# q of two attention tiles in single passes from the split tiles, the projection in q's bank

## The chip, the core and the metric

The kernel runs on one core of a Trainium2 chip, in one launch. The metric is the device time in microseconds from launch to end. The median of three runs of the kernel before is 2429.7 us (2426.54 to 2429.95).

## The reference

x has the shape 8 x 256 x 56 x 56 in float32. Two layers are applied, each with a residual around it and a group normalisation of 32 groups in front:

```
x = x + conv3x3(gn(x))          # 256 -> 256 channels
x = x + attention(gn(x))
```

The attention works in windows of 4 x 4 tokens. For each window:

```
qkv = qkv_w @ x                              # 768 channels, 16 tokens
msq = concat(qkv, avg_pool5(qkv))            # 64 heads of 3*8
q, k = relu(...), relu(...); v = pad(v, 1.0)
kv  = k^T v ; out = q kv ; out = out[:-1] / (out[-1] + 1e-15)
y   = batch_norm(proj_w @ out)
```

avg_pool5 is a 5 x 5 sum around each token inside its window of 4 x 4, over 25.

## The kernel before

All five engines run a program of their own, written out by hand; they meet only at semaphores. Each engine takes its instructions strictly in the order written, and a wait holds up all that stands behind it.

**Convolution.** Each image is done in 4 chunks of 14 rows, each chunk in 4 products (`product`, L332). A product is, for each half of the output channels, 18 matmuls of 392 columns: every operand is split into a high and a low part that TensorE takes in one pass (type float32r), and high x high, high x low and low x high are added. The first chunk of the next image, and a few products after it, are laid between the attention's setup and its last turns.

**Attention.** The 196 windows of an image are cut into 25 tiles of 8 windows, 128 tokens (the last tile has 4 windows). TensorE goes through them in turns s = 0 to 24 (`tile`, L429). Turns 1 to 20 are a hardware loop of ten rounds with two turns each. A turn s does, in this order:

- `attend` for tile s (L405), q times the masked kv, into BANK_O;
- `keys_times_values` for tile s+1 (L391);
- `q_of_tile` for tile s+2 (L371): plain float32 from xh, the normalised tile, into BANK_Q. A float32 matmul is two instruction pairs, so a tile has 8 matmul instructions of 128 columns;
- `turn`, the transposes of tile s (L425), from ao into BANK_O;
- `pooled` for tile s+2 (L380), the 5 x 5 sums of keys and values as a matmul over tokens, into BANK_KV;
- `project` for tile s-1 (L416), 16 matmul instructions of 128 columns, into columns from Y0 on of BANK_A and BANK_A+1;
- `keys_values` for tile s+3 (L364): 6 single passes of 512 columns from xt (the split tile) and wkv, into BANK_KV. It waits for xh_low (the tile's low part) and for vp_raw, ScalarE's last copy of the pooled product out of that bank.

ScalarE goes through `attention` (L703) in turns of the same number: pooled_q for tile s+1 (L678, waits for GpSimd's qsum), turned for tile s (L698, the transposes out of BANK_O), pooled_keys_values for tile s+2 (L652, L655; L655 signals vp_raw), q_of_tile for tile s+2 (L662 copies q to qraw, L666 writes relu(q) to qs straight from the bank), batch_norm for tile s-1 (L690), split_tile for tile s+4 (L632, the high part of xt), keys_values for tile s+3 (L639, L642, L644).

VectorE per turn: the reciprocals and outputs of tile s (L989, L991, L999), the low part of keys and values (L981), two masks of kv (L1008), normalising tile s+4 into xh (L968) and its low part (L976).

GpSimd per turn: spread_pooled for tile s+2 (L1171, waits for vp_raw), pool_q for tile s+2 (L1142 to L1161, eight additions that sum q over 5 x 5 neighbours, waits for qraw; the last one signals qsum_ready), add_tile for tile s-1 (L1182, the residual).

`at_slot` puts nops in front of a stage so that it begins at a given place of TensorE's instruction fetch block.

## Time and profile before

| | before |
|---|---|
| median of the runs | 2429.7 us |
| profiled execution | 2429.06 us |
| its span, first to last instruction | 2427.2 us |
| TensorE busy | 2367.6 us, 98% |
| VectorE busy | 1730.9 us, 71% |
| ScalarE busy | 1453.5 us, 60% |
| GpSimd busy | 1180.7 us, 49% |
| mean granted TensorE clock | 0.998 |

PE is TensorE's matmuls, PEld its weight loads, DVE is VectorE, ACT is ScalarE, POOL is GpSimd. A matmul's end is modelled, so a block's length is best taken from its start to the next block's start. Busy shares are means over stages with different limits. A small wait that ends last in a repeated turn counts more than a large one beside it.

### The profile page before, as it was taken

The page shows a single profiled execution, that of the slowest core. Times are in us where ns is not written, and L with a number is a line of the kernel's source. Part 1 is how long each engine was busy: PE and PEld are TensorE (multiplying, and loading weights), DVE is VectorE, ACT ScalarE, POOL GpSimd, SP SyncE. Part 2 cuts the span into 40 slices and gives each one's busy share as a digit, 9 for nine tenths or more (in the row PEclk, how much of TensorE's full clock was granted, in tenths as well). Part 3 has the DMA queues.
Part 4 walks back from the last instruction along what each step waited for, and adds up shares of the span by engine and source line. Part 5 has one row for each costly group of instructions (what it writes and reads, how often), then busy time and mean ns, then how long its engine had stood idle before and what let it go on. Part 6 is the DMA issues. An engine that isn't in the chain of part 4 may idle for free.

```text
span 2427.2 us, 112385 instructions
## 1 busy us (share of the span) xinstructions
PE 2367.6 (98%) x49576; PEld 2152.7 (89%) x49576; DVE 1730.9 (71%) x3202; ACT 1453.5 (60%) x3756; POOL 1180.7 (49%) x2371
## 2 busy tenths in 40 slices
PE   6999999999999999999999999999999999998998
PEld 6998889888898889988899888998889988897887
DVE  8887658776587675877658766687766876664764
ACT  2148861588615885168841788327882288813886
POOL 2027760377504774047730577206771167712776
PEclk9999999999999999999999999999999999999999
DMA  4000010000100002000010000100001000000000
GB/s 170 1 2 16 16 67 12 2 16 19 65 10 2 19 16 74 1 6 16 19 70 1 6 19 16 71 1 10 16 20 66 1 9 19 21 9 1 16 16 25
DMA packets 38826, 58.37 MB, mean 24 GB/s; under 512 B 4672, under 2 KB 36032, under 8 KB 36288
## 3 DMA queue, kind: packets, MB, share of 16 engines
q1 hardware_dynamic: 38592, 55.27, 6.4%
q8 instruction: 144, 2.36, 0.4%
q14 instruction: 90, 0.74, 0.1%
HBM read 29.57 MB, written 25.69 MB: 23 GB/s over the span
## 4 chain that ended last, share of the span: by engine, by line
PE 96%; DVE 2%; issue 1%; DMA 0%; ACT 0%; POOL 0%; SPq 0%; POOLq 0%; DVEq 0%
PE ps L345 34%; PE ps L416 15%; PE ps L364 11%; PE ps L405 10%; PE ps L391 9%; PE ps L371 9%; PE ps L380 4%; PE ps L425 3%; PE ps L327 0%; DVE dp L875 0%; DVE st L1073 0%; DMA xs<-x 0%; PE ps L356 0%; DVE kv_part L981 0%; DVE rcp L991 0%
## 5 line engine op out<-in xcount | busy, mean ns | idle before, releaser
L345 PE MATMUL ps<-dp,wc 128*128 128x392 f32 x4608 | 842.4, 342 | 4.0 <-issue 4.0
L345 PEld LDWEIGHTS ps<-dp,wc 128*128 128x128 f32 x4608 | 816.9, 188 | 9.2 <-issue 7.6
L1171 POOL TENSOR_TENSOR ve<-vpraw,vmask 128x1024 f32<-128x1024 f32 x200 | 381.0, 1905 | 352.8 <-ACT vpraw L655 352.8
L416 PEld LDWEIGHTS ps<-at,wp 128*128 128x128 f32 x3200 | 373.2, 192 | 48.3 <-DVE kvm L1008 46.4
L416 PE MATMUL ps<-at,wp 128*128 128x128 f32 (+1 forms) x3200 | 404.6, 280 | 1.7 <-ACT yb L690 1.0
L626 ACT CAST dp<-dt 128x896 fp32r<-128x896 f32 x128 | 121.1, 946 | 463.2 <-PE ps L345 374.5
L1142 POOL TENSOR_TENSOR qm<-qraw 128x64 f32<-128x64 f32 x200 | 59.6, 298 | 687.3 <-ACT qraw L662 686.8
L364 PE MATMUL ps<-wkv,xt 128*128 128x512 f32 x1200 | 324.6, 406 | 1.6 <-issue 1.6
L644 ACT ACTIVATE ve<-ps,vmask 128x256 f32<-128x256 f32 x800 | 315.0, 492 | 0.0
L405 PEld LDWEIGHTS ps<-kvm,qs 64*32 64x32 f32 x25088 | 233.6, 105 | 91.4 <-issue 89.6
L1008 DVE TENSOR_TENSOR kvm<-ps,hm 128x576 f32<-128x576 f32 (+1 forms) x400 | 277.5, 735 | 2.9 <-PE ps L391 2.9
L968 DVE TENSOR_SCALAR xh<-xs,gn 128x128 f32<-128x128 f32 (+3 forms) x560 | 278.3, 551 | 1.6 <-PE ps L371 1.3
L405 PE MATMUL ps<-kvm,qs 64*32 64x36 f32 x25088 | 260.7, 204 | 18.3 <-issue 17.7
L976 DVE TENSOR_TENSOR xt<-xh,xt 128x256 fp32r<-128x256 f32 x200 | 108.2, 541 | 236.4 <-ACT xt L632 236.3
L888 DVE TENSOR_TENSOR xs<-xs,ps 128x392 f32<-128x392 f32 x384 | 200.3, 557 | 99.1 <-PE ps L345 98.4
L1182 POOL TENSOR_TENSOR xs<-yb,xs 128x128 f32<-128x128 f32 (+3 forms) x560 | 201.8, 387 | 114.6 <-ACT yb L690 114.6
L391 PE MATMUL ps<-ve,kr 64*32 64x144 f32 x12544 | 246.3, 285 | 1.0 <-issue 1.0
L364 PEld LDWEIGHTS ps<-wkv,xt 128*128 128x128 f32 x1200 | 211.8, 189 | 37.5 <-issue 2.6
L678 ACT ACTIVATE qs<-qsum,qmaskp 128x256 f32<-128x256 f32 x400 | 182.2, 504 | 88.1 <-POOL qsum L1161 88.1
L371 PEld LDWEIGHTS ps<-xh,wq 128*128 128x128 f32 x1600 | 194.4, 191 | 43.3 <-issue 41.3
L989 DVE TENSOR_SCALAR den<-ps 128x64 f32<-128x64 f32 (+1 forms) x200 | 44.5, 223 | 261.5 <-PE ps L405 261.5
L371 PE MATMUL ps<-xh,wq 128*128 128x128 f32 x1600 | 230.2, 287 | 0.0
(86 smaller groups left out, 3121.1 us busy)
## 6 DMA issues: line engine op xcount, KB each, us to landing
out<-xs SPq DMA_DIRECT2D x224, 112.0 KB, 1.8
xs<-x SPq DMA_DIRECT2D x14, 1344.0 KB, 7.5
xs<-x SPq DMA_DIRECT2D x2, 1568.0 KB, 8.4
xs<-x SPq DMA_DIRECT2D x14, 224.0 KB, 2.7
xs<-w_conv SPq DMA_DIRECT2D x2, 1152.0 KB, 13.3
kvm<-w_kv SPq DMA_DIRECT2D x1, 512.0 KB, 14.9
wp<-w_proj SPq DMA_DIRECT2D x4, 128.0 KB, 9.5
wq<-w_q SPq DMA_DIRECT2D x1, 256.0 KB, 14.3
```

What stands on the lines that cost most here:

```text
L345: last = nc.tensor.matmul(ps[:, conv_bank(v, mt), 0:CONV_N], wc[:, part_w, k, kt * TAPS + dy, mt * P:(mt + 1) * P], dp[:, kk % 2, part_d, ...
L364: last = nc.tensor.matmul(ps[0:TT, BANK_KV, :], xt[:, part_x, e, kt, :], wkv[:, part_w, kt, :], start=(i == 0 and kt == 0), stop=(i == len ...
L371: last = nc.tensor.matmul(ps[:, BANK_Q, mt * TT:(mt + 1) * TT], wq[:, kt, mt * P:(mt + 1) * P], xh[:, e, kt, :], start=(kt == 0), stop=(kt ...
L391: last = nc.tensor.matmul(ps[32 * q:32 * q + 32, BANK_A + 2 * h + r, gg * PLACES * QW:(gg + 1) * PLACES * QW], kr[64 * r:64 * r + 64, e, k ...
L405: last = nc.tensor.matmul(ps[32 * c:32 * c + 32, BANK_O + r, (u * G + g) * QW:(u * G + g + 1) * QW], qs[64 * r:64 * r + 64, g, e, w * 32:w ...
L416: last = nc.tensor.matmul(ps[:, BANK_A + mt, Y0:Y0 + n], wp[:, q, mt * P:(mt + 1) * P], at[:, q, e, 0:n], start=(q == 0), stop=(q == QUADS ...
L644: last = nc.scalar.activation(ve[:, t % 2, e, 0].rearrange("p (n m) -> p n m", m=DIM + 1)[:, :, 0:DIM], ps[0:TT, BANK_KV, C:2 * C].rearran ...
L888: last = nc.vector.tensor_tensor(pair[:, :, e], pair[:, :, e], ps[:, conv_bank(v, mt), 0:CONV_N], op)
L968: last = nc.vector.tensor_scalar(xh[:, t % 2, kt, first * TOK:(first + n) * TOK].rearrange("p (w r c) -> p w r c", r=WS, c=WS), xs_row(b, ...
L1008: nc.vector.tensor_tensor(kvm[:, h, 0:n].rearrange("p r (g c) -> p r g c", g=2), ps[:, BANK_A + 2 * h:BANK_A + 2 * h + n, 0:2 * PLACES * Q ...
L1171: nc.gpsimd.tensor_tensor(ve[:, t % 2, :, 1].rearrange("p e (n m) -> p e n m", m=DIM + 1)[:, :, :, 0:DIM], vpraw[:].rearrange("p (n m) -> ...
L1182: last = nc.gpsimd.tensor_tensor(xrow, yb[:, t % 2, mt, first * TOK:(first + n) * TOK].rearrange("p (w r c) -> p w r c", r=WS, c=WS), xrow ...
```

## The change

- q is computed for a pair of tiles at a time, in single passes like keys and values: 3 part combinations x 2 input halves x 2 output halves, 12 matmuls of 256 columns a pair. Its inputs are the split tiles xt, which are laid out so that the two tiles of a pair stand side by side, and wq, which is split into a high and a low part at the start. An image has 13 pairs; in the last only 64 tokens are computed.
- TensorE computes q in even turns, at the place where it was; in odd turns the projection stands at that place, ahead of the transposes. In even turns the projection stays behind pooled. In turn 24 the convolution's product moves behind the transposes.
- The projection writes into BANK_Q. It waits until ScalarE has copied q out of that bank, and q_of_pair waits for batch_norm's y_ready.
- ScalarE copies a pair's q to qraw (128x512) in q_of_pair, and writes relu(q) to qs for each tile from qraw. In even turns its order is pooled_q, q_of_pair, turned, pooled_keys_values, q_of_tile, batch_norm; in odd turns it is pooled_q, q_of_tile, batch_norm, turned, pooled_keys_values.
- GpSimd's pool_q runs once a pair, over buffers of twice the width; spread_pooled stays once a tile, and in even turns pool_q still stands behind it.
- The convolution's products use other banks in two places, and three of the fetch offsets are other numbers.

```diff
@@ conv_bank
     if (c, kk) == (1, 0):
-        return (BANK_KV, BANK_Q)[mt]
-    if (c, kk) == (1, 2):
-        return BANK_O + mt
+        return (BANK_KV, BANK_C[0][1])[mt]
...
-SLOT_LEAD, SLOT_FIRST, SLOT_LOOP, SLOT_OUT = 152, 80, 92, (80, 56)
+SLOT_LEAD, SLOT_FIRST, SLOT_LOOP, SLOT_OUT = 160, 80, 92, (88, 40)
...
-        wq = sb("wq", [P, KT, C])
+        wq = sb("wq", [P, 2, KT, C], F32R)
...
-        xt = sb("xt", [P, 2, 2, KT, TT], F32R)
-        qraw = sb("qraw", [P, MT * TT])
+        xt = sb("xt", [P, 2, KT, 2, TT], F32R)
+        qraw = sb("qraw", [P, MT * 2 * TT])
...
-            def q_of_tile(e):
+            def q_of_pair(tokens=2 * TT):
                 for mt in range(MT):
-                    for kt in range(KT):
-                        last = nc.tensor.matmul(ps[:, BANK_Q, mt * TT:(mt + 1) * TT],
-                                                wq[:, kt, mt * P:(mt + 1) * P], xh[:, e, kt, :],
-                                                start=(kt == 0), stop=(kt == KT - 1))
+                    for i, (part_w, part_x) in enumerate(PARTS):
+                        for kt in range(KT):
+                            last = nc.tensor.matmul(
+                                ps[:, BANK_Q, mt * 2 * TT:mt * 2 * TT + tokens],
+                                wq[:, part_w, kt, mt * P:(mt + 1) * P],
+                                xt[:, part_x, kt, :, :].rearrange("p e t -> p (e t)")[:, 0:tokens],
+                                start=(i == 0 and kt == 0), stop=(i == len(PARTS) - 1 and kt == KT - 1))
                 last.then_inc(q_done, 1)
...
@@ project
-                        last = nc.tensor.matmul(ps[:, BANK_A + mt, Y0:Y0 + n],
+                        last = nc.tensor.matmul(ps[:, BANK_Q, mt * TT:mt * TT + n],
...
@@ tile
-                elif is_tile(2):
-                    pe.wait_ge(q_ready, n2)
-                    q_of_tile(e)
...
+                if e == 0:
+                    if is_tile(2) and s != 0:
+                        if is_tile(3):
+                            pe.wait_ge(xh_low, n4)
+                        pe.wait_ge(y_ready, n0)
+                        q_of_pair(2 * TT if is_tile(3) else TT // 2)
+                elif is_tile(-1):
+                    pe.wait_ge(qraw_ready, pairs)
+                    if is_tile(-2):
+                        pe.wait_ge(y_ready, n0)
+                    project(1 - e, 2)
+                if half and s == TILES - 2:
+                    pe.wait_ge(masked, masks)
                     product(*half)
                 pe.wait_ge(ao_ready, n1)
                 turn(units(0))
...
+                if half and s == TILES - 1:
+                    product(*half)
+                if e == 0 and is_tile(-1):
+                    if is_tile(2):
+                        pe.wait_ge(qraw_ready, pairs)
                     else:
                         pe.wait_ge(y_ready, n0)
                     project(1 - e, 2)
...
@@ scalar
                 if t >= 2:
                     act.wait_ge(kv_done, b * TILES + t - 1)
+                    act.wait_ge(q_done, b * PAIRS_Q + t // 2)
...
+            def q_of_pair(b, i):
+
+                n = 2 * TT if 2 * i + 1 < TILES else TT // 2
+                act.wait_ge(q_done, b * PAIRS_Q + i + 1)
+                if i >= 1:
+                    act.wait_ge(qsum_ready, b * PAIRS_Q + i)
+                nc.scalar.copy(qraw[:].rearrange("p (m n) -> p m n", m=MT)[:, :, 0:n],
+                               ps[:, BANK_Q, :].rearrange("p (m n) -> p m n", m=MT)[:, :, 0:n]).then_inc(qraw_ready, 1)
+
             def q_of_tile(b, t):
 
-                act.wait_ge(q_done, b * TILES + t + 1)
-                if t >= 1:
-                    act.wait_ge(qsum_ready, b * TILES + t)
-                nc.scalar.copy(qraw[:], ps[:, BANK_Q, 0:MT * TT]).then_inc(qraw_ready, 1)
+                act.wait_ge(qraw_ready, b * PAIRS_Q + t // 2 + 1)
...
             def pooled_q(b, t):
 
-                act.wait_ge(qsum_ready, b * TILES + t + 1)
+                act.wait_ge(qsum_ready, b * PAIRS_Q + t // 2 + 1)
...
                     if s + 1 < TILES:
                         pooled_q(b, s + 1)
-                    if s >= 0:
-                        turned(b, s)
-                    if 0 <= s < TILES - 2:
-                        pooled_keys_values(b, s + 2)
-                    if s + 2 < TILES:
-                        q_of_tile(b, s + 2)
-                    if s >= 1:
-                        batch_norm(b, s - 1)
+                    if s % 2:
+                        if 0 <= s and s + 2 < TILES:
+                            q_of_tile(b, s + 2)
+                        if s >= 1:
+                            batch_norm(b, s - 1)
+                        if s >= 0:
+                            turned(b, s)
+                        if 0 <= s < TILES - 2:
+                            pooled_keys_values(b, s + 2)
+                    else:
+                        if 0 < s and s + 2 < TILES:
+                            q_of_pair(b, s // 2 + 1)
+                        if s >= 0:
+                            turned(b, s)
+                        if 0 <= s < TILES - 2:
+                            pooled_keys_values(b, s + 2)
+                        if s == 0:
+                            q_of_pair(b, 1)
+                        if s + 2 < TILES:
+                            q_of_tile(b, s + 2)
+                        if s >= 1:
+                            batch_norm(b, s - 1)
...
@@ gpsimd
-                    if s + 2 < TILES:
-                        pool_q(b, s + 2)
+                    if s % 2 == 0 and s + 2 < TILES:
+                        pool_q(b, s // 2 + 1)
                     if 1 <= s:
                         add_tile(b, s - 1)
```

## Rows read from the trace of the kernel before

**Rows 1.** The page: busy time by engine, and the chain by engine and line.
```profile
PE 2367.6 (98%) x49576; PEld 2152.7 (89%) x49576; DVE 1730.9 (71%) x3202; ACT 1453.5 (60%) x3756; POOL 1180.7 (49%) x2371
...
PE 96%; DVE 2%; issue 1%; DMA 0%; ACT 0%; POOL 0%; SPq 0%; POOLq 0%; DVEq 0%
PE ps L345 34%; PE ps L416 15%; PE ps L364 11%; PE ps L405 10%; PE ps L391 9%; PE ps L371 9%; PE ps L380 4%; PE ps L425 3%; PE ps L327 0%; DVE dp L875 0%; DVE st L1073 0%; DMA xs<-x 0%; PE ps L356 0%; DVE kv_part L981 0%; DVE rcp L991 0%
```

**Rows 2.** Timeline, TensorE, a looped turn: start us, busy us, engine, line, count.
```profile
277.84 1.30 PE L405 MATMUL ps<-kvm,qs 64*32 64x36 f32 x128
...
280.14 1.16 PE L371 MATMUL ps<-xh,wq 128*128 128x128 f32 x8
...
281.13 0.60 PE L425 MATMUL ps<-idn,ao 128*128 128x128 f32 x4
...
281.49 0.71 PE L380 MATMUL ps<-kv_part,poolm 128*128 128x512 f32 x2
...
282.04 2.04 PE L416 MATMUL ps<-at,wp 128*128 128x128 f32 x16
...
283.83 1.61 PE L364 MATMUL ps<-wkv,xt 128*128 128x512 f32 x6
...
285.38 1.30 PE L405 MATMUL ps<-kvm,qs 64*32 64x36 f32 x128
```

**Rows 3.** Timeline, ScalarE and GpSimd, the same stretch; in brackets idle before.
```profile
284.12 0.81 ACT L690 ACTIVATE yb<-ps,bns,bni 128x128 f32<-128x128 f32 x2 [0.22 <-PE ps L416]
...
284.86 0.30 POOL L1142 TENSOR_TENSOR qm<-qraw 128x64 f32<-128x64 f32 x1
...
285.49 0.59 ACT L639 CAST kv_part<-ps 128x512 fp32r<-128x512 f32 x1 [0.27 <-PE ps L364]
...
287.84 0.42 POOL L1161 TENSOR_TENSOR qsum<-qsum,qh 128x128 f32<-128x128 f32 x1
...
288.30 0.91 ACT L678 ACTIVATE qs<-qsum,qmaskp 128x256 f32<-128x256 f32 x2 [0.47 <-POOL qsum L1161]
...
289.11 0.63 ACT L698 COPY at<-ps 128x256 f32<-128x256 f32 x2
...
289.79 0.39 ACT L652 ACTIVATE kr<-ps 128x256 f32<-128x256 f32 x1
290.07 0.38 ACT L655 ACTIVATE vpraw<-ps 128x256 f32<-128x256 f32 x1
...
290.58 0.86 ACT L666 ACTIVATE qs<-ps,qmask 128x256 f32<-128x256 f32 x2
```

**Rows 4.** Timeline, TensorE, a product and what follows it.
```profile
357.59 3.47 PE L345 MATMUL ps<-dp,wc 128*128 128x392 f32 x18
360.90 0.38 PE L425 MATMUL ps<-idn,ao 128*128 128x128 f32 x2
```

**Rows 5.** Groups by line and shape, GpSimd: busy us, mean ns of one, idle before.
```profile
L1171 POOL TENSOR_TENSOR ve<-vpraw,vmask 128x1024 f32<-128x1024 f32 x200 | 381.0, 1905 | 352.8 <-ACT vpraw L655 352.8
...
L1161 POOL TENSOR_TENSOR qsum<-qsum,qh 128x128 f32<-128x128 f32 x200 | 84.9, 425 | 15.7
```

**Rows 6.** Timeline, TensorE, the first two looped turns of an image.
```profile
474.97 0.63 PE L405 MATMUL ps<-kvm,qs 64*32 64x36 f32 x49 [1.35 <-issue]
...
487.37 0.74 PE L380 MATMUL ps<-kv_part,poolm 128*128 128x512 f32 x2 [0.66 <-DVE kv_part L981]
```

**Rows 7.** Timeline, TensorE, the last turn of the last image.
```profile
2417.99 0.44 PE L425 MATMUL ps<-idn,ao 128*128 128x128 f32 x2 [1.13 <-DVE ao L999]
```

**Rows 8.** Timeline beside windows (length, busy, PEclk) of TensorE, around two idle times.
```profile
39.99 2.19 PE L345 MATMUL ps<-dp,wc 128*128 128x392 f32 x11 [1.51 <-issue]
...
38.00:42.00 4.00, 2.49 (x14) 1.00 0.96 390
...
2212.00 0.39 PE L356 MATMUL ps<-mv,gav 128*128 128x2 f32 x2 [2.36 <-DVE mv L800]
...
2212.00:2216.00 4.00, 4.00 (x13) 0.58 0.00 0
```

More of the change, by code:

```diff
@@ L427, in turn, with tile @@
                     last.then_inc(tr_done, 1)
-            def tile(T, e, s=None, v=None):
+            def tile(T, pair, e, s=None, v=None):
                 def is_tile(d):
@@ L439, in tile @@
                 n0, n1, n2, n3, n4 = [held(pe, T + d) for d in range(5)]
-                masks, own_mask = held(pe, T * 2 + 2), held(pe, T * 2 + 3)
+                masks, pairs = held(pe, T * 2 + 2), held(pe, pair + 1)
+                half = None if v is None else {0: (v - 1, 1), TILES - 3: (v, 0), TILES - 2: (v, 1),
+                                               TILES - 1: (v + 1, 0)}.get(s)
                 pe.wait_ge(w_loaded, DMA)
@@ L474, in tile @@
                     pooled(n3)
-                if half and s == 0:
-                    pe.wait_ge(conv_added, 2 * v + 4)
-                    q_of_tile(e)
-                if is_tile(-1):
-                    if is_tile(1):
-                        pe.wait_ge(masked, own_mask)
+                if s == 0:
+                    if half:
+                        pe.wait_ge(conv_added, 2 * v + 4)
+                    pe.wait_ge(xh_low, n4)
+                    pe.wait_ge(qraw_ready, pairs - 1)
+                    q_of_pair()
+                if half and s == TILES - 1:
[3 more added lines that the diff above has]
+                        pe.wait_ge(qraw_ready, pairs)
                     else:
@@ L502, in attention @@
                 v = (b + 1) * CONV_STEPS + len(PRODUCTS) if b + 1 < B else None
-                pe.wait_ge(q_ready, t0 + 1)
-                q_of_tile(1)
+                p0 = b * PAIRS_Q + 1
                 if b + 1 == B:
@@ L514, in attention @@
                 for s in range(FIRST_LOOPED):
-                    tile(t0 + s, s % 2, s, v)
+                    tile(t0 + s, p0 + s // 2, s % 2, s, v)
                 at_slot(SLOT_LOOP)
@@ L522, in attention @@
                         at_slot(SLOT_OUT[s - FIRST_LOOPED - LOOPED])
-                    tile(t0 + s, s % 2, s, v)
+                    tile(t0 + s, p0 + s // 2, s % 2, s, v)
             def last_tile(b):
@@ L552, in later_chunks @@
                             continue
-                        if b >= 1 and (c, kk) == (2, 0):
-                            pe.wait_ge(y_ready, b * TILES + 1)
                         product(v, 0)
@@ L740, in first_chunk @@
                 keys_values(b, 0)
-                q_of_tile(b, 0)
                 pooled_keys_values(b, 0)
                 split(v + 4)
+                q_of_pair(b, 0)
                 split_tile(b, 2)
                 keys_values(b, 1)
+                for t in range(2):
+                    q_of_tile(b, t)
                 pooled_keys_values(b, 1)
@@ L768, in _ @@
             act.wait_ge(c_loaded, CONSTS * DMA)
-            nc.scalar.copy(wkv[:, 0], wkv_raw).then_inc(att_w_high, 1)
+            nc.scalar.copy(wkv[:, 0], wkv_raw)
+            nc.scalar.copy(wq[:, 0], wq_raw).then_inc(att_w_high, 1)
             nc.scalar.copy(poolm[:], poolm_raw).then_inc(y_ready, 1)
@@ L783, in _ @@
                     keys_values(b, 0)
-                    q_of_tile(b, 0)
                     pooled_keys_values(b, 0)
+                    q_of_pair(b, 0)
                     split_tile(b, 2)
                     keys_values(b, 1)
+                    for t in range(2):
+                        q_of_tile(b, t)
                     pooled_keys_values(b, 1)
@@ L1155, in pool_q @@
                 pool.wait_ge(q_step, 6 * n + 4)
-                if t >= 1:
-                    pool.wait_ge(qp_ready, n)
+                if i >= 1:
+                    pool.wait_ge(qp_ready, b * TILES + 2 * i)
                 nc.gpsimd.tensor_tensor(srow[:, :, 3, :], mid, row_[:, :, 3, :], ALU.add).then_inc(q_step, 1)
@@ L1201, in _ @@
             for b in range(B):
+                spread_pooled(b, 0)
                 pool_q(b, 0)
-                spread_pooled(b, 0)
                 spread_pooled(b, 1)
-                for s in range(-1, TILES):
-                    if 0 <= s < TILES - 2:
+                for s in range(TILES):
+                    if s < TILES - 2:
                         spread_pooled(b, s + 2)
-                    if s + 2 < TILES:
-                        pool_q(b, s + 2)
+                    if s % 2 == 0 and s + 2 < TILES:
+                        pool_q(b, s // 2 + 1)
                     if 1 <= s:
```

64 lines of the change are left out of this document (32 added, 32 removed).

## The prediction

> **What bounds the kernel now.** I began with the busy times and the chain that ended last [rows 1]: TensorE is busy for 98% of the span and 96% of the chain is its work, with q (L371) at 9%, the projection (L416) at 15%, keys and values (L364) at 11%. So the first question is how many TensorE microseconds the change takes out. The second is read from TensorE's order of work in one looped turn [rows 2]: 7.54 us with no idle time, in the order attend and keys times values (0 us), q (2.30), transposes (3.29), pooled (3.65), projection (4.20), keys and values (5.99), next turn (7.54). Turns 3 to 20 of each image look like this; two turns are 15.1 us. The third is the other engines' timeline in that turn [rows 3], where the slack of each wait is read. Three waits matter here, all times from the turn's start at 277.84:
>
> - TensorE's keys and values block waits for the copies of the pooled product out of its bank (L652, L655; semaphore vp_raw). L655 ends at 5.07 (290.07 + 0.38 in the next turn, which starts at 285.38), the block starts at 5.99: slack 0.92 us. It is the projection's 1.79 us, issued between pooled and this block, that makes it.
> - ScalarE's pooled_q (L678) waits for GpSimd's qsum (L1161), which lands 3.40 us after that pool pass began (L1142 at 284.86 to 288.26). ScalarE stood idle for it by 0.47 us [rows 3]. It costs nothing today, because ScalarE's next work, turned (L698 at 289.11), waits for the transposes anyway.
> - GpSimd's pool pass starts only after the 1.9 us spread (L1171), itself after L655.
>
> **The change, part by part.** *q on TensorE.* Before: 8 matmul instructions of 128 columns a tile, each with its load, 0.99 us [rows 2], for two tiles 1.98. After: 12 single-pass ones of 256 columns a pair. The trace has no 256-column one. A block of 18 single passes of 392 columns takes 3.31 us (357.59 to 360.90) [rows 4], one of 6 with 512 columns 1.55 [rows 2]. At the full clock of 2.4 GHz the columns alone are 2.94 and 1.28 us, so a block carries some 0.3 us besides. 12 x 256 columns are 1.28 us; I take 1.6. Bounds: 12 x 0.112 (the projection's 1.79/16) = 1.35 us from below, 12 x 0.26 (1.55/6) = 3.1 from above. A pair so saves 0.38 us of TensorE.
>
> *The even turn* (q of the pair, transposes, pooled, projection, keys and values) is 7.54 - 0.99 + 1.60 = 8.15 us. The projection now shares q's bank and waits for the raw copy, 128x512, 0.59 us as L639 [rows 3]; it lies under transposes and pooled (0.91 us). It also stands before turned on ScalarE; q's end is seen there at about 3.95 and the transposes' at 4.3, so turned starts some 0.1 us late and the pooled copies, which wait for TensorE's pooled, not at all: L655 ends at 5.07 + 0.61 = 5.68.
>
> *GpSimd.* Spread 5.75 to 7.67, then the pool pass over twice the width from 7.63. It is eight instructions in 3.40 us [rows 3]. From L1161 (128 elements, 425 ns) and L1171 (1024, 1905 ns) [rows 5] an element costs 1.65 ns and an instruction 0.21 us besides; eight times that is 1.7 us, and of the other 1.7 some is hand-over between instructions that wait for one another, so I take 1.4 us as what doubles. The pass is 3.40 + 1.4 = 4.8 us and qsum lands at 12.43. Bounds: 3.4 (width free) and 6.8 (doubled). Per pair GpSimd works less; what counts is that one pass is later than today: 4.3 us into the odd turn (from 8.15), where it was 2.9.
>
> *The odd turn.* On TensorE: attend and keys times values 2.30, projection 1.79, transposes 0.36, pooled 0.55, so keys and values could start 5.00 us in, at 13.15, with nothing left between pooled and it. On ScalarE the order is now pooled_q (waits for qsum), q_of_tile, batch_norm, turned, pooled_keys_values. All are in line: turned and the pooled copies, which used to start when TensorE was done, are now queued behind the wait for GpSimd. Their lengths [rows 3] are 0.91 + 0.86 + 0.81 + 0.65 + 0.28 (L652's start to L655's) + 0.38 = 3.89, less some 0.1 for each of four seams where they overlap: 3.5. From 12.48 they end at 15.98, TensorE starts keys and values at 16.03 instead of 13.15, a stall of 2.9 us, and the pair ends at 17.58. Against 15.11 that is +2.47 us. What is late next: at_ready (turned ends at 15.4) is before the next attend, the spread for the next even turn ends 0.5 us into it and is wanted at 1.7, ScalarE's split and VectorE's low part of the tile (L632, L976) end before the turn does. So nothing further piles up and the loop is periodic.
>
> Such odd turns are 3, 5, ..., 21: ten an image, 80 in all, 80 x 2.47 = 198 us.
>
> *The edges of each image.* q of tiles 0 and 1 leaves, one pair comes in: -0.4. Turn 0 has a pair's q: +0.6. Turn 1 loses q (-1.0); its attend already has 1.35 us of issue gap [rows 6], so TensorE comes to keys and values 6.35 us in, and ScalarE's line, from a qsum at some 4 us, ends at 7.5: +1.1. In turn 2, q's 0.6 us more cover a wait for kv_part that is 0.66 [rows 6]: -0.6. Turn 22's q of 64 tokens still has 12 loads, 12 x 0.112 + 0.1: +0.4. Turn 24 has no product left between attend and its transposes; the last image shows what is then bare, 1.13 us of waiting for ao [rows 7], and its attend waits for turned(23) by another 0.9, for the projection that covered it has moved ahead: +2.0. Sum +2.1 us, 17 over eight images. The splitting of wq at the start (a copy and a subtraction of 512) is under the first products.
>
> *The clock.* TensorE has next to no idle time today. Where it had some: after 2.36 us (before 2212.00) the next 4 us ran at a mean granted clock of 0.58, that is 3.4 of them at the lower of its two levels, 1.2 instead of 2.4 GHz; after 1.51 us (before 39.99) it stayed at 1.00 [rows 8]. A stall of 2.9 us is longer than the one after which it fell. One fall costs at most 3.4 x 0.5 = 1.7 us, and what is slowed is keys and values and the even turn, both on the path. Between none and 80 x 1.7 = 136 us I take 0.8 us a stall, 64 us, since part of a fall will lie in idle time and some stalls may bring none.
>
> The Trainium skill, "TensorE: Matmul & The Clock Gate", section "Why this matters for your kernels", asks for no idle gaps above about 3 us between bursts of matmuls. By that rule the stalls here would leave the clock alone and the time would be 2644. The trace does not agree: 2.36 us was enough [rows 8].
>
> **The sum.** The profiled execution took 2429.06 us (span 2427.2), and the median of the runs is 2429.7, so no correction: 2429 + 198 + 17 + 64 = 2708, say 2710.
>
> **The rivals.**
> 1. *GpSimd is not what binds*, because the wider pass costs less than I think or is overtaken. Then the odd turn goes by ScalarE after the projection: it ends at 8.15 + 2.30 + 1.79 = 12.24, batch_norm starts 0.29 later (284.12 against 283.83 [rows 2, 3]), then 0.81 + 0.65 + 0.28 + 0.38 less 0.2 gives 14.45, and the pair ends at 16.05: +0.94, 75 us, no fall of the clock (stall 1.35). 2429 + 75 + 17 = 2521. For it: it needs only a pass under about 3.3 us. Against it: 3.4 is what half the width takes.
> 2. *The width is paid in full*: pass 6.8 us, pair 19.6, +4.47: 2429 + 358 + 17 + 64 = 2868. For it: several of the eight step over every fourth element, and the trace has no long instruction of that kind. Against it: L1161 and L1171 [rows 5].
> 3. *Faster*: the stall doesn't come, and the pair is 15.11 + 1.60 - 1.98 = 14.73, 80 x -0.38 + 17 = -13: 2416. Its place is vp_raw of the odd turn, its condition that L655 ends by 13.1, 2.9 us before my figure. With ScalarE's 3.5 us after it, qsum would have to land at 9.6, 2.0 us after the pool pass starts; and ScalarE's way after the projection alone is 1.35 too late. This speaks hard against it; for it only that the unstalled engine work does shrink.
> 4. *The new q is dearer than its parts*: at 3.1 us a pair, +1.5 us x 80 more: 2828.
> 5. *The clock* falls never (2644) or each time (2780); both are inside the range.
>
> **How the numbers follow.** Forecast with its clock ends: 0.76. Rival 1: 0.09. Rival 2: 0.05. Rival 4: 0.03. Rival 3: 0.05. No change: 0.02, for parts that happen to cancel. 0.2% (5 us) is about what a measurement of this kernel can tell from none. Range: a pass of 4.3 us without falls of the clock gives 2604, one of 5.3 with all of them 2820; widened for the edges and q's block to 2575 and 2835. Left out are rivals 1, 2 and 3. Faster 0.05, same 0.02, slower 0.93.
>
> **What would show it.** TensorE's idle time before L364 some 2.5 to 3 us in odd turns, put down to ScalarE's vpraw; none in even turns. ScalarE's pooled_q waiting for GpSimd's qsum in every odd turn, some 1.5 to 2 us, and turned starting long after the transposes. q's line 12 matmuls in 1.6 us. Pairs of turns 17.6 us apart. Granted clock below 1.00 in the attention stages. Wrong: pairs under 16 us, or keys and values without idle time before it; then a path on ScalarE is shorter than I read, or GpSimd's pass hardly grows.

## The result, and the profile after

| | before | after |
|---|---|---|
| median of the runs | 2429.6 us | 2757.0 us (2748.0 to 2759.4, 4 runs) |
| ratio, 95% interval | 1 | 1.134 (1.132 to 1.136) |
| profiled execution, its span | 2429.06, 2427.2 us | 2755.4, 2753.5 us |
| mean granted TensorE clock | 0.998 | 0.947 |

The change costs 327 us, 13.4%. 2710 was predicted, with a range of 2575 to 2835.

The page of the changed kernel: the busy times, the chain that ended last by engine, and three groups of instructions (busy us, mean ns of one, idle time before them and what ended it).
```profile
PE 2450.7 (89%) x49224; PEld 2195.7 (80%) x49224; DVE 1745.1 (63%) x3203; ACT 1416.9 (51%) x3661; POOL 1057.7 (38%) x1603
...
PE 87%; issue 10%; DVE 2%; ACT 0%; POOL 0%; DMA 0%; SPq 0%; POOLq 0%; DVEq 0%
...
L363 PE MATMUL ps<-wkv,xt 128*128 128x512 f32 x1200 | 382.8, 461 | 228.7 <-issue 228.7
...
L1017 DVE TENSOR_TENSOR xt<-xh,xt 128x256 fp32r<-128x256 f32 x200 | 212.2, 1061 | 424.3 <-ACT xt L645 424.2
...
L700 ACT ACTIVATE qs<-qsum,qmaskp 128x256 f32<-128x256 f32 (+1 forms) x400 | 183.0, 516 | 205.7 <-POOL qsum L1203 205.6
```
Against [rows 1]: TensorE's share of the chain falls from 96% to 87%, and "issue" rises from 1% to 10%. Nearly all of TensorE's new idle time stands ahead of one line, keys and values (L363; it was L364), and nearly all of ScalarE's wait for GpSimd ahead of pooled_q (L700; it was L678). TensorE's busy time went up, not down, although the single-pass q takes less time. That is the lower clock: a mean of 0.947 is some 292 us of the span (0.053 / 0.5 x 2753.5) at the lower of its two levels, 1.2 instead of 2.4 GHz. (Line numbers have moved: projection L419, q L372, pooled L383, transposes L428, product L344.)

The timeline of TensorE over one even and one odd turn, and the start of the next two.
```profile
605.50 1.39 PE L408 MATMUL ps<-kvm,qs 64*32 64x36 f32 x128
606.73 1.23 PE L394 MATMUL ps<-ve,kr 64*32 64x144 f32 x64
607.89 1.69 PE L372 MATMUL ps<-xt,wq 128*128 128x256 f32 x12
609.42 0.60 PE L428 MATMUL ps<-idn,ao 128*128 128x128 f32 x4
609.77 0.71 PE L383 MATMUL ps<-kv_part,poolm 128*128 128x512 f32 x2
610.32 1.99 PE L419 MATMUL ps<-at,wp 128*128 128x128 f32 x16
612.06 1.64 PE L363 MATMUL ps<-wkv,xt 128*128 128x512 f32 x6
613.63 1.30 PE L408 MATMUL ps<-kvm,qs 64*32 64x36 f32 x128
614.79 1.23 PE L394 MATMUL ps<-ve,kr 64*32 64x144 f32 x64
615.95 2.05 PE L419 MATMUL ps<-at,wp 128*128 128x128 f32 x16
617.84 0.60 PE L428 MATMUL ps<-idn,ao 128*128 128x128 f32 x4
618.19 0.72 PE L383 MATMUL ps<-kv_part,poolm 128*128 128x512 f32 x2
621.59 1.71 PE L363 MATMUL ps<-wkv,xt 128*128 128x512 f32 x6 [2.68 <-issue]
623.24 1.60 PE L408 MATMUL ps<-kvm,qs 64*32 64x36 f32 x128
624.61 2.08 PE L394 MATMUL ps<-ve,kr 64*32 64x144 f32 x64
...
640.33 2.90 PE L363 MATMUL ps<-wkv,xt 128*128 128x512 f32 x6 [2.70 <-issue]
```
The even turn lasts 8.13 us without idle time, q's twelve matmuls 1.53 (607.89 to 609.42). In the odd turn TensorE has nothing to do for 2.7 us after pooled. The profile calls the wait "issue", because it finds no releaser for it. In the code two waits stand ahead of L363. One is for the tile's low part, which VectorE had ready at 613.95. The other is for the copies out of the pooled bank, and the other engines' timeline of the same stretch shows when they end.
```profile
613.25 0.42 POOL L1184 TENSOR_TENSOR qm<-qraw 128x128 f32<-128x128 f32 x1
...
617.31 0.67 POOL L1203 TENSOR_TENSOR qsum<-qsum,qh 128x256 f32<-128x256 f32 x1
...
618.01 0.91 ACT L700 ACTIVATE qs<-qsum,qmaskp 128x256 f32<-128x256 f32 x2 [1.94 <-POOL qsum L1203]
...
619.62 0.78 ACT L713 ACTIVATE yb<-ps,bns,bni 128x128 f32<-128x128 f32 x2
620.30 0.63 ACT L721 COPY at<-ps 128x256 f32<-128x256 f32 x2
620.82 0.40 ACT L665 ACTIVATE kr<-ps 128x256 f32<-128x256 f32 x1
621.09 0.40 ACT L668 ACTIVATE vpraw<-ps 128x256 f32<-128x256 f32 x1
```
Read from bottom to top it is one queue, called ScalarE's file from here on: L668 ends at 621.49, 0.10 us before keys and values start. Everything from L700 on is queued on ScalarE without a gap, and L700 itself waited 1.94 us for the last instruction of GpSimd's pass. The projection that L713 reads was done by 617.84 and the transposes that L721 reads by 618.19 (the next blocks' starts), so both stood ready for about 2 us behind instructions that a wait not their own had held back.

The windows of the same turns (length, busy time, granted clock; the last two numbers are DMA): an odd turn, an even one, and the next two.
```profile
613.63:623.24 9.61, 6.93 (x222) 0.99 0.00 1
623.24:632.37 9.13, 9.13 (x234) 0.83 0.07 25
632.37:643.16 10.79, 8.09 (x222) 0.86 0.00 0
643.16:651.29 8.13, 8.13 (x234) 0.98 0.08 28
```
The clock is lower after each of the two stalls. After the first stall it is attend and keys times values that run long (1.37 and 2.01 us from start to start instead of 1.16), after the next keys and values (2.83 instead of 1.57).

### The profile page after: what moved, and what is told of

Read it like the earlier page. It is cut to its first block, busy times and chain, and to the rows that moved or that the text cites. A ratio compares the mean times of both kernels' runs of the same rounds, so it can differ in the third digit from the quotient of the medians.

```text
span 2753.5 us, 110819 instructions
## 1 busy us (share of the span) xinstructions
PE 2450.7 (89%) x49224; PEld 2195.7 (80%) x49224; DVE 1745.1 (63%) x3203; ACT 1416.9 (51%) x3661; POOL 1057.7 (38%) x1603
## 4 chain that ended last, share of the span: by engine, by line
PE 87%; issue 10%; DVE 2%; ACT 0%; POOL 0%; DMA 0%; SPq 0%; POOLq 0%; DVEq 0%
PE ps L344 30%; PE ps L419 14%; PE ps L363 13%; PE ps L408 9%; PE ps L394 8%; PE ps L372 6%; PE ps L383 4%; PE ps L428 3%; DVE ao L1040 0%; PE ps L326 0%; DVE st L1114 0%; DVE rcp L1032 0%; DMA xs<-x 0%; DVE dp L917 0%; PE ps L355 0%
## 5 line engine op out<-in xcount | busy, mean ns | idle before, releaser
L344 PE MATMUL ps<-dp,wc 128*128 128x392 f32 x4608 | 848.6, 343 | 5.7 <-issue 5.7
L344 PEld LDWEIGHTS ps<-dp,wc 128*128 128x128 f32 x4608 | 824.6, 190 | 9.6 <-issue 7.7
L363 PE MATMUL ps<-wkv,xt 128*128 128x512 f32 x1200 | 382.8, 461 | 228.7 <-issue 228.7
L363 PEld LDWEIGHTS ps<-wkv,xt 128*128 128x128 f32 x1200 | 241.5, 215 | 309.9 <-issue 266.2
L1017 DVE TENSOR_TENSOR xt<-xh,xt 128x256 fp32r<-128x256 f32 x200 | 212.2, 1061 | 424.3 <-ACT xt L645 424.2
L419 PEld LDWEIGHTS ps<-at,wp 128*128 128x128 f32 x3200 | 374.9, 191 | 41.0 <-issue 24.6
L419 PE MATMUL ps<-at,wp 128*128 128x128 f32 (+1 forms) x3200 | 403.6, 279 | 1.5 <-ACT yb L713 1.0
L408 PE MATMUL ps<-kvm,qs 64*32 64x36 f32 x25088 | 273.9, 215 | 27.9 <-issue 21.9
L700 ACT ACTIVATE qs<-qsum,qmaskp 128x256 f32<-128x256 f32 (+1 forms) x400 | 183.0, 516 | 205.7 <-POOL qsum L1203 205.6
L394 PE MATMUL ps<-ve,kr 64*32 64x144 f32 x12544 | 269.7, 305 | 1.0 <-issue 1.0
L652 ACT CAST kv_part<-ps 128x512 fp32r<-128x512 f32 x200 | 117.0, 585 | 221.8 <-PE ps L363 221.7
L394 PEld LDWEIGHTS ps<-ve,kr 64*32 64x32 f32 x12544 | 215.3, 114 | 4.3 <-issue 4.2
L713 ACT ACTIVATE yb<-ps,bns,bni 128x128 f32<-128x128 f32 (+1 forms) x400 | 158.5, 446 | 101.0 <-PE ps L419 100.9
L1009 DVE TENSOR_SCALAR xh<-xs,gn 128x128 f32<-128x128 f32 (+3 forms) x560 | 191.2, 395 | 0.3
```

What stands on the lines that cost most here:

```text
L344: last = nc.tensor.matmul(ps[:, conv_bank(v, mt), 0:CONV_N], wc[:, part_w, k, kt * TAPS + dy, mt * P:(mt + 1) * P], dp[:, kk % 2, part_d, ...
L363: last = nc.tensor.matmul(ps[0:TT, BANK_KV, :], xt[:, part_x, kt, e, :], wkv[:, part_w, kt, :], start=(i == 0 and kt == 0), stop=(i == len ...
L394: last = nc.tensor.matmul(ps[32 * q:32 * q + 32, BANK_A + 2 * h + r, gg * PLACES * QW:(gg + 1) * PLACES * QW], kr[64 * r:64 * r + 64, e, k ...
L408: last = nc.tensor.matmul(ps[32 * c:32 * c + 32, BANK_O + r, (u * G + g) * QW:(u * G + g + 1) * QW], qs[64 * r:64 * r + 64, g, e, w * 32:w ...
L419: last = nc.tensor.matmul(ps[:, BANK_Q, mt * TT:mt * TT + n], wp[:, q, mt * P:(mt + 1) * P], at[:, q, e, 0:n], start=(q == 0), stop=(q == ...
L1009: last = nc.vector.tensor_scalar(xh[:, t % 2, kt, first * TOK:(first + n) * TOK].rearrange("p (w r c) -> p w r c", r=WS, c=WS), xs_row(b, ...
```

## The experiments

Eleven variants of the changed kernel were run. Two theories stood at first. **Mine**: GpSimd's wider pass lands late, ScalarE's queue passes that on to the copies TensorE needs, and the clock falls on top. **The rival**: the projection, now ahead of transposes and pooled, leaves nothing between pooled and keys and values, and ScalarE is simply too long after it whatever GpSimd does. The kernel before took 2429.6 us beside the changed kernel, but 2423.8 beside e1 to e4 and 2424.9 to 2425.4 beside the others. So a difference between the time of the changed kernel and that of a variant is uncertain by some 6 us; each ratio is to the kernel before of the same runs.

### e1, e2, e3: the order on ScalarE

e1 moves pooled_q, the instruction that waits for GpSimd, to the end of ScalarE's odd turn. e2 leaves it first and puts the pooled copies ahead of q_of_tile and batch_norm. e3 does both. e1 and e3, in the odd turn (e2 keeps the first two lines as they were and moves the other two alone):
```
-                    if s + 1 < TILES:
+                    if s % 2 == 0 and s + 1 < TILES:
                         pooled_q(b, s + 1)
                     if s % 2:
-                        q_of_tile(b, s + 2)      # e3 and e2
-                        batch_norm(b, s - 1)     # e3 and e2
                         turned(b, s)
                         pooled_keys_values(b, s + 2)
+                        pooled_q(b, s + 1)       # e1 and e3
+                        q_of_tile(b, s + 2)      # e3 and e2
+                        batch_norm(b, s - 1)     # e3 and e2
```


> The changed kernel, but in odd turns ScalarE's pooled_q (the wait for GpSimd's qsum) stands last, behind pooled_keys_values. Theory (GpSimd's late pass holds turned and the pooled copies back): the stall before keys and values shrinks from 2.9 us to about 1.3, what is left is batch_norm behind the projection; two turns take 16.1 us instead of 18.8 (17.6 at the full clock), the clock stays at 1.00 in the looped turns, and the time is 2757 - 80 x 2.7 = about 2540. Rival (the line of four ScalarE steps binds by itself, GpSimd's wait is hidden in it): no more than 0.3 us a pair, 2730 or above.

> The changed kernel, but in odd turns ScalarE's order is pooled_q, turned, pooled_keys_values, q_of_tile, batch_norm: the wait for GpSimd stays in front, q and batch_norm stand behind. Theory (GpSimd's pass sets the start, ScalarE's steps in line the rest): qsum at 12.5 us from the even turn's start, then 0.9 + 0.65 + 0.66 less overlaps, keys and values at 14.75 instead of 16.1, two turns 16.3 us at the full clock, stall 1.6, few falls of the clock: about 2560. Rival (q_of_tile and batch_norm would fit into idle time anyway): 2700 or above.

> The changed kernel, but in odd turns ScalarE's order is turned, pooled_keys_values, pooled_q, q_of_tile, batch_norm: neither GpSimd nor q nor batch_norm stands in front of the copies. Theory: what is left is the copies themselves (1.41 us from pooled's start to the end of L655 against 0.55 of TensorE's pooled), a stall of 0.85 us a pair that the projection used to cover; two turns 15.6 to 16.0 us, 2500 to 2530, slower than the kernel before (2430) although TensorE has less work. Rival (the stall comes only from the order on ScalarE, the projection's place is free): no idle time before keys and values, two turns 14.8 us, about 2405 to 2415.

Measured: e1 2556.8 us, ratio 1.054 (1.053 to 1.056); e2 2545.7, 1.050 (1.048 to 1.052); e3 2524.2, 1.041 (1.039 to 1.043). The row of keys and values in an odd turn, for the three in turn:
```profile
551.24 1.62 PE L363 MATMUL ps<-wkv,xt 128*128 128x512 f32 x6 [1.13 <-issue]
```
```profile
545.99 1.63 PE L363 MATMUL ps<-wkv,xt 128*128 128x512 f32 x6 [1.21 <-issue]
```
```profile
621.37 1.60 PE L363 MATMUL ps<-wkv,xt 128*128 128x512 f32 x6 [0.79 <-issue]
```
e1 takes GpSimd out of the file ahead of the copies and wins back 200 of the 327 us (194 by the ratios), with the matrix work untouched. Pairs are 16.0 us apart, where rival 1 of the prediction reckoned 16.05 for a GpSimd that doesn't bind: so its mechanism is there, as the next wait behind the one that decided. e2 shortens the file behind the wait instead, and the wait for GpSimd, though it is still there, costs about as little. e3's 0.79 us is what is left when ScalarE has nothing else to do; its timeline of ScalarE in that odd turn:
```profile
619.92 0.65 ACT L721 COPY at<-ps 128x256 f32<-128x256 f32 x2 [2.17 <-PE ps L428]
```
ScalarE is idle for 2.17 us, then copies the transposes and, up to 621.27, the pooled product (L668), and TensorE waits for that. No order on ScalarE hides it: it is the price of an odd turn with no matmul between pooled and keys and values, as e5 goes on to show. Keys and values has no idle time ahead of it in e3's even turns.

### e4: the clock alone

22 matmuls of 224 columns on weights, whose result nothing reads, fill the stall of the looped odd turns. The output is unchanged.
```
+                if s is None and e == 1:
+                    pe.wait_ge(masked, held(pe, T * 2 + 3))
+                    for _ in range(22):
+                        nc.tensor.matmul(ps[...], wkv[:, 0, 0, 0:P], wkv[:, 0, 0, 0:224], start=True, stop=True)
```


> The changed kernel with 22 matmuls of 224 columns into unused columns of a bank between pooled and keys and values in the looped odd turns (80 of 88 stalls): they compute nothing that is used, and take some 2.3 of the 2.9 us of idle time. Theory (a stall costs its idle time and, besides, 1.2 us a pair by the clock that falls to 1.2 GHz after it): no falls in the looped turns, two turns 17.6 instead of 18.8, about 2757 - 90 = 2665, though more TensorE instructions run. Rival (what is slowed at the lower clock lies in idle time or is hidden): 2745 to 2760, or above for the added work.

Measured: 2659.9 us, ratio 1.098 (1.096 to 1.099), mean clock 0.992. TensorE in an odd turn of it:
```profile
598.29 2.61 PE L505 MATMUL ps<-wkv 128*128 128x224 f32 x22
...
601.18 1.62 PE L363 MATMUL ps<-wkv,xt 128*128 128x512 f32 x6 [0.28 <-issue]
```
Pairs are 17.6 us apart, the 9.53 + 8.08 of the changed kernel's pairs in which the clock stays up, and the time is 97 us less (89 by the ratios). So of the 327 us the lower clock is some 90 to 97, 1.1 to 1.2 us for each of the 80 stalls that were filled. The wait itself, 17.6 against 15.11 us a pair, is 178 us in turns 3 to 20 of the eight images; the start and the edges of the images are the rest.

### e5, e6: work back behind pooled

e5 splits the projection of odd turns: the first half of the channels stays ahead of the transposes, the second goes behind pooled. ScalarE has e3's order, and q_of_tile moves into the even turn.
```
-                    project(1 - e, 2)
+                    project(1 - e, 2, (0,))
...
                 if is_tile(2):
                     pooled(n3)
...
+                if e == 1 and is_tile(-1):
+                    project(1 - e, 2, (1,))
```


> From the changed kernel: in odd turns the projection's first half (8 matmul instructions) stands ahead of the transposes and its second half behind pooled; ScalarE's odd order is turned, pooled_keys_values, pooled_q, batch_norm, and q_of_tile for the odd tile stands in the even turn, behind pooled_q. Theory (keys and values stall because the copies of the pooled product have lost the projection's cover; half of it, 0.9 us, is as long as the 0.85 us that was bare): no idle time before keys and values, odd turn 6.6 to 6.8 us, two turns 14.7 to 14.9 against 15.11 before and 15.64 with the copies moved forward alone; from that kernel's 2524 (2429 before: the same runs) 80 x 0.85 less, about 2455. That it is still not below the kernel before would be the edges of each image, 7 us each. Rival (ScalarE with 12.9 us of work in 14.7 becomes the bound): two turns 15.3 or more, 2500.

Measured: 2467.0 us, ratio 1.018 (1.016 to 1.019); 2455 was expected. The odd turn of e5 from the projection's first half on:
```profile
531.20 1.16 PE L419 MATMUL ps<-at,wp 128*128 128x128 f32 x8
532.19 0.60 PE L429 MATMUL ps<-idn,ao 128*128 128x128 f32 x4
532.54 0.72 PE L383 MATMUL ps<-kv_part,poolm 128*128 128x512 f32 x2
533.10 1.05 PE L419 MATMUL ps<-at,wp 128*128 128x128 f32 x8
534.06 1.63 PE L363 MATMUL ps<-wkv,xt 128*128 128x512 f32 x6
```
The 0.96 us of projection covers the 0.79 that e3 left bare, and the stall is gone. The odd turn is 6.7 us, and with an even turn of 8.15 the pair is 14.85, shorter than the 15.11 of before. But four even turns of each image take 8.8 to 9.6 us instead, so the mean pair of turns 3 to 20 is 15.34. That and the edges of the images keep the whole above the kernel before.

e6 adds to e5 that the last turn's product is issued ahead of its transposes, where the waits of 0.6 and 1.1 us of turn 24 lay.
```
-                if half and s == TILES - 2:
+                if half and s >= TILES - 2:
                     pe.wait_ge(masked, masks)
                     product(*half)
...
-                if half and s == TILES - 1:
-                    product(*half)
```


> As the split projection, and in turn 24 the convolution's product stands ahead of the transposes again, as in the kernel before. Theory (the wait for ao in turn 24, the idle time ahead of it and the clock that falls there make up a part of the edges): product(v+1) takes 3.3 us instead of 4.4 to 4.85, and the wait of about 1.1 us goes: 2.0 to 2.8 us less for seven images, 15 to 20 us below the run with the split projection alone, about 2438, within 1% of the kernel before on either side. Rival (those waits are hidden, the next stage starts at a time set by VectorE): within 4 us of the split projection alone.

Measured: 2461.0 us, ratio 1.015 (1.014 to 1.017), 6 us less than e5 where 15 to 20 were expected; the two ratios' intervals overlap, so the traces must decide. In them the stretch from turn 24 to the next turn 0 fell from 108.66 to 107.47 us in the second image, and by as much in all but the seventh (2.6): only the wait went. I had counted a fall of the clock there too, as in the changed kernel, but in e5 the product behind that wait already ran at the full clock.

### e7: GpSimd's order

e7 swaps GpSimd's two jobs that meet at the odd turn in the changed kernel: the pool pass first, the spread of the pooled keys and values behind it.
```
-                    if s < TILES - 2:
-                        spread_pooled(b, s + 2)
                     if s % 2 == 0 and s + 2 < TILES:
                         pool_q(b, s // 2 + 1)
+                    if s < TILES - 2:
+                        spread_pooled(b, s + 2)
```


> The changed kernel, but in even turns GpSimd does pool_q ahead of spread_pooled. Theory (each GpSimd pass is wanted at a time; the pool pass is early now, the spread late): qsum lands about 9.4 us from the even turn's start instead of 12.4, the spread ends at 11.3, while the odd turn's second half of keys times values wants it at 9.8: 1.5 us of idle time there, then 1.4 before keys and values by ScalarE's line behind the projection. Two turns stay at 17.5 us; with two stalls of 1.5 instead of one of 2.9 the clock falls seldom, so about 2670. Rival (only the pool pass is tight, the spread has room): two turns 16.1, about 2545.

Measured: 2730.4 us, ratio 1.126 (1.124 to 1.128); some 2670 was expected. TensorE in an odd turn:
```profile
592.73 0.72 PE L394 MATMUL ps<-ve,kr 64*32 64x144 f32 x32 [1.67 <-POOL ve L1213]
...
597.48 1.63 PE L363 MATMUL ps<-wkv,xt 128*128 128x512 f32 x6 [1.14 <-issue]
```
The mechanism was as expected: the stall for ScalarE is down to e1's 1.14 us, since qsum comes in time, and the spread is now what is late, by 1.67 us in the middle of keys times values. One long stall has become two short ones of about the same sum (2.81), and the pair at 17.85 us is even longer than the changed kernel's 17.6 at full clock. What it gains is the clock (0.982 against 0.947). The size was missed in the pair by 0.3 us, at turn 1, which took some 14 to 15 us with a wait of 3.7 to 4.2 for the spread and the lower clock behind it, and in eight odd turns in which the clock fell all the same (1.3 to 1.6 us more each).

### e8: a second raw buffer

In e5 and e6 the even turns that are too long show it at the projection, which waits for ScalarE's copy of q out of its bank (0.5 to 0.8 us of idle time there). Such a turn of e6, from 564.10 on:
```profile
562.54 2.46 DVE L1013 TENSOR_SCALAR xh<-xs,gn 128x96 f32<-128x96 f32 x3
...
568.36 0.93 ACT L688 ACTIVATE qs<-qraw,qmask 128x256 f32<-128x256 f32 x2
...
569.40 0.58 ACT L678 COPY qraw<-ps 128x512 f32<-128x512 f32 x1
```
The copy (L678) stands behind q_of_tile of the odd tile (L688), which must read the single qraw before it is overwritten. ScalarE is late in this turn, because the tile's high part waited for VectorE's normalising (L1013), which took 2.46 us for three instructions beside GpSimd's spread, where four of the same kind take 1.19 in the changed kernel. GpSimd's own pass had been done before. e8 is e6 with two of the buffers:
```
-        qraw = sb("qraw", [P, MT * 2 * TT])
+        qraw = sb("qraw", [P, 2, MT * 2 * TT])
```
and q_of_tile behind the pooled copies in even turns.

> As the split projection with turn 24's product ahead (2461), but with two qraw buffers, so that ScalarE's copy of the pair's q out of the bank need not wait for q_of_tile of the odd tile; that one moves behind pooled_keys_values in even turns. Theory (in some four even turns an image ScalarE comes late to the copy, because VectorE's normalising took 2.5 to 2.8 us beside GpSimd's spread, and TensorE waits 0.65 to 1.45 us at the transposes, pooled and the projection): these waits go or fall under 0.3 us, all even turns take 8.05 to 8.2, 4.4 us an image, 35 in all: about 2430, level with the kernel before within 0.5%. Rival (ScalarE is late as a whole and not at this place): the wait moves to keys and values or to attend, 2450 to 2465.

Measured: 2429.7 us, ratio 1.0014 (1.0005 to 1.0024), as expected. Buffer and order were changed together, so which of the two did it isn't shown. The odd turns take 6.71 us and most even ones 8.05. The mean pair of turns 3 to 20 is 14.86 us against 15.11, 18.6 us less over the eight images, and slightly more is given back at the start and the edges. The dearest is turn 2, in its timeline and the window behind the idle time:
```profile
481.61 1.17 PE L408 MATMUL ps<-kvm,qs 64*32 64x36 f32 x112
484.37 0.30 PE L408 MATMUL ps<-kvm,qs 64*32 64x36 f32 x16 [1.60 <-issue]
```
```profile
485.50:489.50 4.00, 4.00 (x48) 0.62 0.01 4
```
The idle time falls inside a run of 128 equal instructions that wait for nothing, in the first pass through a loop body, as the 1.35 us of [rows 6] did before; the clock falls behind it, as it does in five of the eight images (idle times of 1.58 to 2.12 us).

### e9, e10, e11: where the loop body lies

SLOT_LOOP is the constant by which the program pads the code ahead of the looped turns; 92 became 28, 156 and 220 in e8.

> The two-qraw kernel (2429.7) with the loop's place in the fetch block at 28 instead of 92. There turn 2 of each image takes 11.4 us: 1.6 us of issue gap in attend and, at half the clock after it, 1.0 us more in q and 0.5 in keys times values. Theory (the gap comes where TensorE's instructions are fetched for the first time, its size depends on where the block ends, and the clock's part on its size): other places move 1 to 3 us an image, 10 to 25 us in all, either way. Rival (the place in the block is without effect here): 2430 within 4 us.

> The two-qraw kernel with the loop's place at 156. Theory: 10 to 25 us off 2430 either way; if it holds, one of the three places 28, 156 and 220 is below 2425, the kernel before. Rival: 2430 within 4 us.

> The two-qraw kernel with the loop's place at 220. Theory: 10 to 25 us off 2430 either way, the difference found in turns 1 and 2 of each image. Rival: 2430 within 4 us.

| | slot | median, us | ratio (95%) | turns 1 and 2 of the second image, us |
|---|---|---|---|---|
| e9 | 28 | 2428.7 | 1.0018 (1.0009 to 1.0028) | 7.20 and 9.90 |
| e8 | 92 | 2429.7 | 1.0014 (1.0005 to 1.0024) | 6.75 and 11.37 |
| e10 | 156 | 2432.6 | 1.0034 (1.0021 to 1.0046) | 8.82 and 9.32 |
| e11 | 220 | 2438.6 | 1.0057 (1.0040 to 1.0073) | 7.76 and 9.80 |

The gap moves between the two turns, but never leaves. The medians lie within 9 us of e8's where 10 to 25 either way had been expected; e9 and e10 are within the 4 us of the rival, for which the place is without effect, and only e11 is outside it. One slot below the kernel before had been expected, and there was none. No version here beats that kernel: e8 and e9 come to 0.2% of it.

## Why the prediction was right

**q on TensorE.** 1.6 us a pair forecast, 1.53 measured, far from the upper bound (3.1), so rival 4 is out. **The even turn**: 8.15 forecast, 8.13 measured, with no wait for the shared bank.

**GpSimd.** A pass of 4.8 us forecast, 4.73 measured (613.25 to 617.98), qsum at 12.48 us from the even turn's start against 12.43. The share that doubles, 1.4 us worked out from two instructions of [rows 5], can be added up from the means of the eight by shape: 3.08 us before, 4.49 after, 1.41 more. Twice the width costs under half as much again: the last addition takes 425 ns at 128 elements and 715 at 256, so 128 elements more cost 290 ns and some 135 ns don't grow. Rival 2 (6.8 us) fails there. By these two an element costs 2.3 ns and not the 1.65 of the prediction, which took a longer instruction for the second point. Its fixed part of 0.21 us was too large, and its total came out right all the same because part of the rest was set aside as hand-over.

**The odd turn.** ScalarE's file: 3.5 us forecast, 3.48 measured (618.01 to 621.49); keys and values at 16.09 us against 16.03; the pair where the clock stays up 17.61 (8.08 and 9.53) against 17.58. These are rows of the second image at full clock; over all images the wait is the same 2.7 us in each of the 72 odd turns from 3 to 19. That the file is what binds was argued from the trace alone and is shown by e1 and e2, which leave the matrix work as it is and win 200 and 211 us. Rival 1 and rival 3 are shown false for the change as it stands, and true of what lies behind it: e1 is rival 1's loop, and the undisturbed pairs of e5 and e8 are rival 3's (14.85 and 14.76 us; it reckoned 14.73), once the wait is gone. The prediction's condition for it, that the copies end 2.9 us earlier, took both a new order on ScalarE and half of the projection put back.

**The clock.** This term was mis-sized most in microseconds. 0.8 us for each of 80 stalls, 64 us, was forecast as if part of them would bring no fall; e4 measures 89 to 97, 1.1 to 1.2 each. The mean pair between turns 3 and 20 is 18.75 us, 1.16 more than e4's, and the clock fell behind 65 of the 72 stalls there. The range had both ends (0 and 136). The Trainium skill, "TensorE: Matmul & The Clock Gate", section "Why this matters for your kernels", asks for no gap above about 3 us. The trace disagrees again: the stalls here are 2.7 us, and e8's fall came after 1.60.

**The edges.** 2.1 us an image forecast, 4.4 measured when turn 21 is counted as the forecast did, and the parts are less well met than the sum. Turns 0 to 2 grew by 2.1 us an image where 0.1 was forecast: in turn 1 the sum of q came 4.85 us in and not 4, so the stall is 2.8 to 3.2 us in seven images instead of 1.15, and the clock falls behind it. Turn 21 was counted as a full stall with its clock, 3.3 us; its stall is only 1.3 to 1.75, without a fall, and it grew by 1.2. Turns 22 to 24 with what follows them grew by 4.3 us where 2.0 was forecast. So one miss hides part of the others, and that is luck. Turn 24 of the first image shows what was left out:
```profile
398.85 0.76 PE L408 MATMUL ps<-kvm,qs 64*32 64x36 f32 x64 [0.61 <-ACT at L721]
400.74 0.44 PE L428 MATMUL ps<-idn,ao 128*128 128x128 f32 x2 [1.13 <-DVE ao L1040]
400.93 5.00 PE L344 MATMUL ps<-dp,wc 128*128 128x392 f32 x18
```
The two waits are the 0.9 and 1.13 that were forecast (0.61 and 1.13). But the product behind them takes 4.84 us, start to start, instead of the 3.31 of [rows 4], at a granted clock of 0.65. So it is in four of seven images; in the other three the product takes 3.3 us. Some 0.7 us of idle time at the start of turn 0 was under q of tile 1 before. The forecast treated the edges as waits only and gave them no clock.

**The start.** The splitting of wq was said to be under the first products. It isn't: VectorE's subtraction stands ahead of the work that the convolution waits for.
```profile
37.20 0.68 DVE L1133 TENSOR_TENSOR wq<-at,wq 128x512 fp32r<-128x512 f32 x1
```
The product that started at 39.99 [rows 8] starts at 40.53, the granted clock is 0.50 from 40 to 46 us where it was 1.00, and the first turn of attention starts 3.7 us later than before. The 0.54 us of the restart are the subtraction's; that the clock fell because of it isn't shown.

**The sum.** The profiled execution is 326 us longer, where 278 was forecast. Of the 48 us between them 26 lie in turns 3 to 20 (261.6 against 235), nearly all of it clock. 16 lie in turns 0 to 2 and 4 at the start. Turns 21 to 24 with what follows them are only 2 above the forecast, because turn 21 cost less than said and the rest more.

## What to carry to other kernels

An engine executes in order: before moving an instruction that waits for another engine, write down what is queued behind it and who wants that, because the wait is paid there and not where the profile first shows it. TensorE was idle for ScalarE's copy, and the cause was GpSimd, two steps further back. A kernel whose chain is nearly all TensorE has its slack in the pieces between one matmul block's end and the next block that reads what was copied out of it; moving 1.8 us of matmuls out of such a place needs 1.8 us of slack there, and here there were 0.92. Each stall that opens should be priced with the clock that it loses as well (here 1.2 us more for one of 2.7), and so should a short instruction that is added where the first products are waiting.

## What the runs showed of the hardware

**Idle times and the clock.** In the looped odd turns from 3 to 19 (72 a run) the clock fell behind 65 of the idle times of 2.7 us, behind 8 of e7's of 1.2 to 1.7, and behind none of 1.2 (e2), 1.13 (e1) and 0.79 (e3). In e8's turn 2 it fell after five of eight between 1.58 and 2.12, after one of 1.60 but not after one of 1.87. The kernel before had kept it after 1.51 [rows 8]. So the length of the gap alone doesn't decide: gaps of one length did both.

**VectorE beside GpSimd.** VectorE's low part of the tile (L1017) takes 0.42 us where no GpSimd instruction runs beside it (22 tiles of the changed kernel), 0.47 in the even turn below, and four times that beside GpSimd's spread. Timeline of the changed kernel, an even and an odd turn:
```profile
613.48 0.47 DVE L1017 TENSOR_TENSOR xt<-xh,xt 128x256 fp32r<-128x256 f32 x1 [2.58 <-ACT xt L645]
...
621.57 1.89 POOL L1213 TENSOR_TENSOR ve<-vpraw,vmask 128x1024 f32<-128x1024 f32 x1 [2.76 <-ACT vpraw L668]
621.82 1.93 DVE L1017 TENSOR_TENSOR xt<-xh,xt 128x256 fp32r<-128x256 f32 x1 [2.28 <-ACT xt L645]
```
It starts 0.25 us behind the spread and ends 0.29 us after it, as if it had stood still until the spread was done and then run for two thirds of its time alone. The even turn's has the same mark: it ends 0.28 us after GpSimd's short L1184, which ran to 613.67. The variants bear this out, since they move the two against each other. In e1 the same instruction starts 1.04 us behind the spread:
```profile
551.21 1.89 POOL L1215 TENSOR_TENSOR ve<-vpraw,vmask 128x1024 f32<-128x1024 f32 x1 [0.92 <-ACT vpraw L668]
552.25 1.13 DVE L1019 TENSOR_TENSOR xt<-xh,xt 128x256 fp32r<-128x256 f32 x1 [1.88 <-ACT xt L645]
```
In e8 it starts 1.33 us behind and takes 0.84 (medians). In all three it ends 0.28 to 0.29 us after the spread does, however early it began. In e2 it starts only 0.15 us before the spread's end, and takes 0.43. The mean over all turns is 541 ns in the kernel before, 1061 in the changed one and 462 in e2. Here it costs nothing: the tile's first reader is q, 2.9 us later (623.75 to 626.62). The Trainium skill, "SBUF — State Buffer", section "Who interferes with whom", says that an instruction of VectorE with two inputs in SBUF contends with one of GpSimd that reads SBUF, and that the ports they share are an exclusive lock; the rows agree.

**Equal instructions, unequal starts.** In the first passes through the looped code (turns 1 and 2) TensorE pauses in the midst of a block whose instructions wait for nothing, whichever slot the loop begins at: 0.8 to 1.4 us in the kernel before, 1.6 to 2.1 in e8, and in e10 and e11 in both turns, up to 2.2 each. The profile can name nothing that it waits for. That code is being fetched would fit; it was not tested by itself.
